# A decoder block on one core: the prologue in another order, two projections moved ahead of the first step, one rotation given to GpSimd

## The reference

```python
x = _layernorm(x + _L0_attn_ref(x, ...))          # linear attention, 32 heads of 8
x = _layernorm(x + _L0_xattn_ref(x, ctx, ctx, pos, pos, ...))  # softmax attention, 16 heads of 16
x = _layernorm(x + _L0_ffn_ref(x, ...))           # 256 -> 64 -> 1024 -> gelu -> 64 -> 256
```

## Time and profile before

| what | us |
|---|---|
| median of three executions | 535.34 |
| their lowest and highest | 535.23, 536.82 |
| the profiled execution's own time | 537.56 |
| its span, first to last instruction | 535.8 |
| TensorE (matmul) busy | 498.2 (93%) |
| VectorE busy | 400.5 (75%) |
| ScalarE busy | 312.7 (58%) |
| GpSimd busy | 344.5 (64%) |
| mean granted TensorE clock | 0.974 |

### The profile page before, as it was taken

The page is one execution under the profiler, slowest core; times in us unless marked ns, Lnnn a source line. Parts: engine busy times, 40 slices in busy tenths (PEclk is TensorE's granted clock), DMA queues, the critical chain, the costliest instruction groups (busy, mean ns, idle before and its releaser), DMA issues.

```text
span 535.8 us, 11400 instructions
## 1 busy us (share of the span) xinstructions
PE 498.2 (93%) x4044; PEld 336.6 (63%) x4044; DVE 400.5 (75%) x878; ACT 312.7 (58%) x457; POOL 344.5 (64%) x391
## 2 busy tenths in 40 slices
PE   6997799999999999999999999999978788999992
PEld 3885566677676767676777767777745333645451
DVE  6567877888888888888888888878887765545453
ACT  3543266665657574748475656666566577565650
POOL 6649245867777778686877777787676425342525
PEclk9899899999999999999999999999989789999997
DMA  8663203020402040213202220302000001133332
GB/s 268 143 117 91 73 12 86 11 65 11 104 13 83 16 100 24 74 38 81 85 13 49 69 85 11 100 16 65 11 24 22 16 21 60 69 107 112 125 108 108
DMA packets 29132, 36.01 MB, mean 67 GB/s; under 512 B 5721, under 2 KB 15321, under 8 KB 29081
## 3 DMA queue, kind: packets, MB, share of 16 engines
q1 hardware_dynamic: 28216, 34.37, 22.4%
q10 hardware_dynamic: 864, 0.95, 0.7%
HBM read 23.51 MB, written 8.65 MB: 60 GB/s over the span
## 4 chain that ended last, share of the span: by engine, by line
PE 74%; issue 10%; DVE 6%; POOL 5%; ACT 3%; DMA 1%; POOLq 1%; SPq 0%; ACTq 0%
PE FR L1223 22%; PE BK L1223 12%; PE BK L1401 11%; PE SC L1382 6%; PE SC L1350 6%; PE FR L1310 4%; PE FR L1302 3%; PE FR L1287 3%; PE FR L1427 2%; POOL rs L648 2%; POOL c_fm L653 2%; PE SC L1223 2%; DVE nmax L1038 2%; PE SC L1587 1%; ACT probs L756 1%
## 5 line engine op out<-in xcount | busy, mean ns | idle before, releaser
L1038 DVE TENSOR_REDUCE nmax<-SC 128x4 f32<-128x1024 f32 x128 | 155.8, 1218 | 27.3 <-PE SC L1350 24.9
L756 ACT ACTIVATE probs<-SC 128x1024 f32<-128x1024 f32 x128 | 130.9, 1026 | 57.5 <-PE SC L1382 57.4
L1401 PE MATMUL BK<-probs,v_aug 128*32 128x256 f32 x1024 | 70.7, 393 | 1.0 <-ACT probs L756 0.7
L1350 PE MATMUL SC<-k_blk,q_grp 48*128 48x512 f16 x256 | 50.3, 389 | 9.1 <-DVE nmax L1038 8.3
L1382 PE MATMUL SC<-q_grp,k_blk 64*128 64x256 f16 x512 | 50.8, 279 | 5.1 <-ACT probs L756 2.5
L852 ACT ACTIVATE probs<-SC,b_ff 128x512 f32<-128x512 f32 x64 | 38.9, 688 | 25.9 <-PE SC L1592 25.9
L1401 PEld LDWEIGHTS BK<-probs,v_aug 128*32 128x32 f32 x1024 | 26.8, 110 | 28.5 <-issue 12.1
L1382 PEld LDWEIGHTS SC<-q_grp,k_blk 64*128 64x128 f16 x512 | 20.0, 96 | 32.6 <-issue 15.1
L718 ACT ACTIVATE lin_fm_h<-FR 128x512 fp32r<-128x512 f32 x15 | 9.0, 597 | 45.3 <-PE FR L1310 45.3
L648 POOL TENSOR_TENSOR rs<-ve,minus_half 128x2 f32<-128x2 f32 x16 | 11.1, 692 | 35.9 <-DVE nm L1209 35.9
L529 POOL TENSOR_TENSOR att_fm_l<-att_raw,att_fm_h 128x512 fp32r<-128x512 f32 x16 | 20.6, 1287 | 20.3 <-ACT att_fm_h L731 20.3
(11 more groups left out here) (239 smaller groups left out, 1537.1 us busy)
## 6 DMA issues: line engine op xcount, KB each, us to landing
x_fm<-in_x_fm SPq DMA_DIRECT2D x16, 256.0 KB, 5.4
x_tm<-in_x_tm SPq DMA_DIRECT2D x16, 256.0 KB, 5.0
x_kept<-x2b SPq DMA_DIRECT2D x16, 256.0 KB, 2.1
x_tm<-x_kept SPq DMA_DIRECT2D x16, 256.0 KB, 2.7
out<-c_fm SPq DMA_DIRECT2D x16, 256.0 KB, 2.0
c_fm<-in_c_fm SPq DMA_DIRECT2D x15, 256.0 KB, 5.4
tables<-rope_tables SPq DMA_DIRECT2D x16, 128.0 KB
k_blk<-k_rope SPq DMA_DIRECT2D x128, 16.0 KB, 1.8
```

The source lines that it names most:

```text
L756: act.activation(probs[:, j % 4], (SC[j % 2] if b == LAST else SB)[:], ACT.Exp, scale=SCALE).then_inc(s_exp, 1)
L1038: dve.tensor_reduce(nmax[:, t, :, 2 * q:2 * q + 2], src[:].rearrange("p (s f) t -> p s f t", s=2), AX.X, ALU.max, negate=True).then_inc(s_ ...
L1350: mm = pe.matmul(out[:, 2 * s:2 * s + 2].rearrange("p h t -> p (h t)"), q_grp[n % NB][rows, q, t * P:(t + 1) * P], k_blk[n % NB][rows, q]. ...
L1401: mm = pe.matmul(BK[q // 2][HP * k:HP * (k + 1), (q % 2) * T:(q % 2 + 1) * T], v_aug[b % NB][:, t, HC * q + k], probs[:, j % 4, k], start= ...
```

## The change

The computation stays the same. These parts are in another order or on another engine:

- VectorE makes the low parts KV1 and KV1_C1 directly behind the turns (L900), ahead of L903. Q1 and K2 follow L905, V2 follows L909. GpSimd starts `split_c(0)` one low part later.
- ScalarE loads the table of Sin ahead of the first high part, and the three sines stand behind `ev_k2(0)` in place of ahead of `ev_kv1(0)`. TensorE runs `vk(0)` ahead of `k2(0)`.
- SP issues b_o2, x_fm of image 2 and w_o2 ahead of the table writes in place of behind the table reads.
- `k2(2)` and `v2(2)` leave step(0) and stand among the scores of image 0 in the prologue, in FR[0], with their evictions. `x1_t(1)`, `q2(1)` and `lin_t(2)` move to later places there, `lin_t(2)` to BK[1].
- The rotation of image 1's queries leaves VectorE, but for the swap of halves, and becomes GpSimd's `rope_q_cos(1)` and `rope_q(1)`. 
- In step(0) the shift (`shift_t`, `ev_shift`) stands ahead of `scores1(1, 0)` and `row_max(1, 0)`.

```diff
@@ -361,6 +361,10 @@
+            sp.dma_start(b_o2[:], a["b_o2"].unsqueeze(0).broadcast_to([P, C])).then_inc(s_b_o2, 16)
+            load_x_fm(2)
+            stage_in(O2, split[O2][0], "w_o2")
+
             sp.wait_ge(s_tab, 1)
@@ -389,9 +393,6 @@
-            sp.dma_start(b_o2[:], a["b_o2"].unsqueeze(0).broadcast_to([P, C])).then_inc(s_b_o2, 16)
-            load_x_fm(2)
-            stage_in(O2, split[O2][0], "w_o2")
             for h in range(2):
@@ -601,7 +602,7 @@
             split_x(0)
-            pool.wait_ge(s_w_lo, KV1_C1 + 1)
+            pool.wait_ge(s_w_lo, Q1 + 1)
             split_c(0)
@@ -627,6 +628,8 @@
             weights_lo(DD2, s_ff_lo)
+            rope_q_cos(1)
+            rope_q(1)
             residual_bias(2)
@@ -672,13 +675,17 @@
+            act.preload_act_table(ACT.Sin)
             for k in (KV1, KV1_C1, Q1, K2, V2):
...
-            act.wait_ge(s_ang, 8)
-            act.activation(tab[:, 0], red[:, 1], ACT.Sin).then_inc(s_tab, 1)
-            act.activation(tab[:, 1], red[:, 0], ACT.Sin).then_inc(s_tab, 1)
-            act.activation(tab[:, 2], red[:, 0], ACT.Sin, scale=-1.0).then_inc(s_tab, 1)
+            def sines():
+
+                act.wait_ge(s_ang, 8)
+                act.activation(tab[:, 0], red[:, 1], ACT.Sin).then_inc(s_tab, 1)
+                act.activation(tab[:, 1], red[:, 0], ACT.Sin).then_inc(s_tab, 1)
+                act.activation(tab[:, 2], red[:, 0], ACT.Sin, scale=-1.0).then_inc(s_tab, 1)
+
             act.wait_ge(s_ones, 1)
@@ -769,7 +776,7 @@
                 exp_chunk(b, 1)
-                if on(n):
+                if on(n) and b > 0:
                     ev_k2(n, FR[1])
@@ -800,6 +807,7 @@
             ev_k2(0, SA0)
+            sines()
             ev_v2(0, SA1)
@@ -821,10 +829,12 @@
             norm1(1, 1)
+            ev_k2(2, FR[0])
+            ev_x1(1, FR[1])
             weights_hi(DD2)
-            ev_x1(1, FR[1])
-            ev_q2(1)
-            ev_lint(2, FR[1])
+            ev_v2(2, FR[0])
+            ev_lint(2, BK[1])
+            ev_q2(1, FR[1])
             def last_step():
@@ -899,31 +909,30 @@
             ins.then_inc(s_ang, 1)
+            def weights_lo(k):
+                dve.wait_ge(s_w_hi, k + 1)
+                src, hi, lo = split[k]
+                dve.tensor_tensor(lo, src, hi.bitcast(F32), ALU.subtract).then_inc(s_w_lo, 1)
+
+            weights_lo(KV1)
+            weights_lo(KV1_C1)
             dve.wait_ge(s_ang, 3)
...
                                      ALU.mult, ALU.add).then_inc(s_ang, 1)
-
+            weights_lo(Q1)
+            weights_lo(K2)
             dve.wait_ge(s_ang, 5)
             dve.scalar_tensor_tensor(red[:], turns[:], -PI_B, red[:], ALU.mult, ALU.add).then_inc(s_ang, 1)
-            def weights_lo(k):
-                dve.wait_ge(s_w_hi, k + 1)
-                src, hi, lo = split[k]
-                dve.tensor_tensor(lo, src, hi.bitcast(F32), ALU.subtract).then_inc(s_w_lo, 1)
-
-            weights_lo(KV1)
+            weights_lo(V2)
             dve.wait_ge(s_ang, 6)
             dve.scalar_tensor_tensor(red[:], turns[:], -PI_C, red[:], ALU.mult, ALU.add).then_inc(s_ang, 1)
-            weights_lo(KV1_C1)
             dve.wait_ge(s_ang, 7)
...
             dve.tensor_scalar(red[:, 1], red[:, 1], PI_LOW, -PI_LOW, ALU.min, ALU.max).then_inc(s_ang, 1)
-
-            for k in (Q1, K2, V2):
-                weights_lo(k)
@@ -1096,8 +1105,11 @@
+                if b == 0:
+                    ev_shift(b)
                 row_max(n1, 0)
-                ev_shift(b)
+                if b > 0:
+                    ev_shift(b)
                 if on(n):
@@ -1157,14 +1169,13 @@
             row_max(0, 3, SB)
+            row_max(0, 4)
             lin(2, (BK[1], BK[0]))
             ev_x1(1, FR[1])
-            row_max(0, 4)
-            rope_q(1)
-            rope_q_sum(1)
             row_max(0, 5, SB)
-            lint(2, FR[1])
+            lint(2, BK[1])
             row_max(0, 6)
+            q_halves(1)
             row_max(0, 7, SB)
@@ -1233,7 +1244,9 @@
                 pe.wait_ge(s_xs, m + 1)
-                if m >= 3:
+                if m == 4:
+                    pe.wait_ge(s_pvc_ev, 1)
+                elif m >= 3:
                     pe.wait_ge(s_v2_ev, m - 1)
@@ -1265,7 +1278,9 @@
                 pe.wait_ge(s_cs, n + 1)
-                if on(n + 1) and n >= 2:
+                if n == 2:
+                    pe.wait_ge(s_proj_ev, 2)
+                elif on(n + 1) and n > 2:
                     pe.wait_ge(s_kv1_ev, 2 * (n + 1) + 1)
@@ -1273,7 +1288,9 @@
-                if n >= 2:
+                if n == 2:
+                    pe.wait_ge(s_k2_ev, 3)
+                elif n > 2:
                     pe.wait_ge(s_pvc_ev, n - 1)
@@ -1356,7 +1373,7 @@
                     pe.wait_ge(s_w_rest, 16 * N_W_REST)
-                    pe.wait_ge(s_q2_ev, 2)
+                    pe.wait_ge(s_v2_ev, 3)
                 pe.wait_ge(s_shift, b + 1)
@@ -1430,10 +1447,13 @@
+                if b == 0:
+                    shift_t(b)
                 scores1(n1, 0)
...
                     scores2(p, 7)
-                shift_t(b)
+                if b > 0:
+                    shift_t(b)
                 if on(m):
@@ -1500,9 +1520,9 @@
             q1(0)
+            vk(0, out=BK[1])
             pe.wait_ge(s_w_lo, K2 + 1)
             k2(0, SA0)
-            vk(0, out=BK[1])
             pe.wait_ge(s_w_lo, V2 + 1)
@@ -1538,15 +1558,18 @@
             scores1(0, 3)
-            x1_t(1, FR[1])
+            k2(2, FR[0])
+            scores1(0, 4)
             lin(2, 0, BK[1])
             lin(2, 1, BK[0])
-            scores1(0, 4)
-            q2(1)
+            x1_t(1, FR[1])
             scores1(0, 5)
-            lin_t(2, FR[1])
+            v2(2, FR[0])
+            lin_t(2, BK[1])
             scores1(0, 6)
+            q2(1, FR[1])
             scores1(0, 7)
+            pe.wait_ge(s_q2_ev, 2)
             proj1(2)
```

## The result

| | kernel before | changed kernel | predicted |
|---|---|---|---|
| median, us | 536.06 (4 runs, 535.23 to 536.82) | 542.80 (4 runs, 540.66 to 543.87) | 529.1 |
| ratio | 1 | 1.0109, interval 1.0073 to 1.0145 | 0.988 |
| profiled execution, us | 537.56, span 535.8 | 541.74, span 539.9 | 531.3 |

A forecast was written before the change was run, and what follows sets the result against it. It took TensorE, and the chain over it, to bound the kernel, with idle or half-clock stretches at the start and among the scores. 3.3 - 0.3 + 2.8 + 0.45 = 6.25 us off the 535.34 median gave 529.1 us, range 527.6 to 532.0.

The forecast's parts named there:

- part 2: Prologue, sines and tables later: reads issued at 25.0 us, landing in 2.3 us; VectorE waits 0.3 us.
- near the small transfers: Ground for taking 2.3 us as the table read's landing time, since SP issues no bulk just ahead.
- Part 1: Start of the prologue, low parts first on VectorE: 1.80 us plus 1.5 us from the clock, 3.3 us gained.
- this shift of 3.3 us goes through images 0 and 1: Prologue: the start's gain is passed on, TensorE being busy almost without a gap, if the tables allow it.
- 1.5 us for the clock: First products on TensorE: nine products at full instead of mostly half speed, ends being 0 and 1.5 us.
- Part 3: Scores of image 0, projections moved in, rotation on GpSimd: 2.8 us gained, GpSimd's addition releasing scores1(1, 0).
- the second rival: Score stretch gives back its gain, by GpSimd's work or TensorE's waits lowering the clock: 531.9 us; chance 0.14.
- Part 4: Step 0 without two projections: 0.45 us gained, kv1 to fourth block 4.68 us, set by VectorE's row maximum.
- Slower, the tables: Rival: table write and read both land in 9.2 us, 542.6 us; chance 0.08 (0.05 no change, 0.03 slower).
- the writes landed in 2.6 us: Argument against the slow-tables rival: table writes landed that fast with bulk in flight.
- a slack of -0.3: Tables forecast at 28.0 us, wanted by VectorE at 27.7 us: a 0.3 us wait, passed on.

The follow-up runs named there:

- e3: Changed kernel with the loads of w_v1, w_d2 and c_fm of image 2 issued ahead of the wait for the sines: 543.44 us, ratio 1.0115.
- e6: Changed kernel with bulk loads ahead of sines, vk(0)'s mask ahead of angle operations, GpSimd behind them, ScalarE issuing four table writes: 541.21 us, ratio 1.0070.
- e8: e6 without GpSimd's wait for the angle operations: 543.35 us, ratio 1.0103.
- e4: Changed kernel with VectorE's mask of vk(0) ahead of the last four angle operations: 543.61 us, ratio 1.0100.
- e11: e4 with the first two images' tables filled with the constant 0.7, so nobody waits for a read: 534.78 us, ratio 0.9949.
- e10: The kernel of e1 measured once more: 535.52 us, ratio 0.9965 against the kernel before.
- e1: Changed kernel with the old start put back, the edits among the scores and in step 0 kept: 535.63 us, ratio 0.9975.
- e7: Kernel before with only the three sines moved behind ev_k2(0) and the Sin table loaded first: 542.08 us, ratio 1.0088.
- e9: e1 with the rotation of image 1's queries back on VectorE: 536.53 us, ratio 0.9989.

## Why the prediction was wrong

| step | predicted, us | measured, us |
|---|---|---|
| first product; `q1(0)` | 10.55; 13.4 | 10.42; 13.29 |
| eviction of `k2(0)` | 17.7 | 17.33 |
| first sine | 18.3 | 20.26 |
| table reads issued | 25.0, 25.7 | 27.04, 27.72 |
| tables there | 28.0 | 33.88 |
| `lin(1)` | 29.7 | 37.73 |
| `scores1(0, 0)` | 37.9 | 47.37 |
| `kv1(3, 0)` | 58.7 | 68.54 |
| from it to the fourth block | 4.68 | 4.69 |

**The step that failed is part 2, in the landing of the table read.** It was sized at 2.3 us, "near the small transfers", between 1.9 and 9.2 us. It takes 4.3 us with no bulk behind it (e3, e6, e8) and 6.2 with it. Before, 9.0 us lay between the second read's issue (21.25 plus some 0.7 us) and its use at 30.96, and hid it whole. The prediction's ground, that SP issues no bulk just ahead of the reads, looked the wrong way for 1.9 of the 3.9 us: what is issued behind them counts. The other 2.0 are the read's own, and no row of before had them. Along the chain, the landing is 3.9 of the 9.8 us between forecast and measurement at `kv1(3, 0)`. Had it alone come true, VectorE would still have come to the tables at 30.80 us, so that only 3.1 us would have been won there.

**Part 2's second fault is the first sine**, 2.0 us late. Its time was read off ScalarE's list, but the sines also need the angles. Part 1 had costed VectorE's move at the durations of before, when no subtraction or addition of GpSimd's ran beside the angles. The trace of before had the warning: there the low part of K2 took 1.77 us beside GpSimd's split, the low part of Q1 ahead of it 0.67.

**What was missing.** Behind the tables, two of VectorE's operations stretch in the same way (1.46 and 1.48 us for 0.42), 2.1 us; and the idle time of 5.23 us brings the half clock, 1.5 us by the time of `scores1(0, 0)`. Together 2.0 + 3.9 + 2.1 + 1.5 = 9.5 us, and 0.3 in the scores: 9.8. Behind step 0 0.6 us more, which makes up the spans' difference to the forecast, 539.9 - 529.6 = 10.3 us. The mask of `vk(0)`, queued behind the angles, was not seen; it eats 3 us at `lin(0)` with the half clock behind it, which the tables would have taken anyway (e4).

**Part 1** was right in its marks (first product, spacing, clock 1.00), and worth little: its step "this shift of 3.3 us goes through images 0 and 1" failed even without the tables (e11: `k_cos` at 29.06 us, forecast 27.7). The marks were good ones besides: in the eight profiles with the new start `q1(0)` starts between 13.29 us (the changed kernel's) and 14.46 us (e8, where the high part of the second KV1 piece begins at 11.39 us). Its 1.5 us for the clock were read off one profiled execution, and they come and go from one to the next. With the old order of the first products, q1(0) came 4.39 and 4.41 us behind the first product in two profiles (before, e10) and 2.87 or 2.88 in three (e1, e7, e9). The idle time ahead of the first product was 2.75 and 2.83 us in the two, and 1.81 to 2.26 us in the three, so the clock may hang on when the weights land; no run sets that time by itself. A saving read off a half clock in one profile should have been taken at some half of it. The Trainium skill (TensorE: Matmul & The Clock Gate, Part 1: The HAM clock gate) says of a kernel's first products that how many run slow varies between runs of one kernel. These profiles, e1 and e10 above all, which are one kernel, show such a variation behind an idle time too.

**Part 3** came out at 2.54 us for 2.8 in this profile. Its release was named wrongly: VectorE's shift, not GpSimd's addition, 0.05 us apart. And that profile flatters it. In the nine others the wait of some 2 us that it brings is followed by half speed, and the stretch gains 1.4 us (23.71 - 22.34, e1). That is the clock half of the second rival ("TensorE's waits ... could lower the clock"), which takes back 1.2 of the 2.8 us. **Part 4** was right in size and release: 4.69 us, VectorE's row maximum. From the first score block to the fourth block of step 0 it is 27.07 us in e1 and in e10, 28.84 before: 1.8 us for the two parts, and e10's median agrees (0.35% of 537.16 is 1.9 us, with an interval of 1.0 to 2.8). e1's profile stands 3.3 us ahead of before's at `lin_t(3)` (77.12 against 80.42): 1.4 and 0.4 from these parts, and 1.5 from a start that in e1 had its full clock.

**The rival.** "Slower, the tables" was the right mechanism, even its price (542.6 us) close, for another mixture: later issue, 6.2 us in place of 9.2, and two costs it didn't hold. That the price came so close is luck. It was given 3 in 100 on the slower side because "the writes landed in 2.6 us". The writes did land (in 1.9 us); the evidence was about the writes, and the read had none. A cost with bounds of 1.9 and 9.2 us and a slack of -0.3 deserved far more of the chance.

**Open.** A shorter table path was not tried: fewer and larger writes, or low parts made on another engine so that the angles come first again. From the first sine to the tables it is 6.8 us to the first read's issue, 0.7 to the second's, and 6.2 landing: 13.6 in all, 11.7 without bulk behind. In this kernel a start earlier than the tables allow is wasted. Whether the 4.3 us come from the read's shape (one row copied to many partitions) was not measured, nor why transfers issued behind a read slow it.

## What to carry to other kernels

A transfer whose landing no row shows because it was hidden is an unknown of the size of its cover: when a change eats the cover, price it at the far bound, or keep the issue where it is. When work on VectorE or GpSimd is moved, ask which of the other's operations will run beside it; small ones may take the other's duration. And a start that is faster by 3 us buys nothing while the next thing wanted by TensorE hangs on a path that was made longer.

## What the runs showed of the hardware that I had not expected

- A 128x256 f32 `TENSOR_SCALAR` on VectorE took 0.29 us alone and 1.27 or 1.36 beside GpSimd's elementwise operations; a 128x32 one 0.18 and 0.77, a `SCALAR_TENSOR_TENSOR` of that size 0.18 and 1.02.
- A table read of 128 KB took 4.3 us with the DMA engines 13 to 20% busy, and 6.2 to 6.5 us with bulk issued behind it. The Trainium skill (DMA: Bandwidth & Descriptors, Anatomy of one DMA) gives some 2.0 us fixed for the GpSimd path plus a size term that is an estimated 0.3 us here. For this read, on SP's queue, the rows show 4.3, and they decide.
- The 32 KB table writes landed in 1.8 to 3.9 us in eleven profiles, and in 6.8 to 7.6 (e6) and 3.1 to 4.4 us (e8) where bulk was issued shortly ahead of them.
- The same first products in the same order ran at full speed in three profiles (behind 1.81 to 2.26 us of idle time) and mostly at half in two (behind 2.75 and 2.83). Behind the same wait of 2.18 us among the scores TensorE went on at 2.4 GHz once and at 1.2 in the eight other profiles that have it.
